# Eight-batch two-layer kernel: the first (gelu) experts run dense for batch 0 only, and by dispatched tiles of 256 token rows for batches 1 to 7

## The chip, the core and the metric

The kernel runs on one NeuronCore of a Trainium2 chip. The metric is device time in microseconds (us) of one execution, from three runs. The profile is one execution taken by the hardware profiler; its times count from the first instruction. PE is TensorE, PEld its weight loads, DVE is VectorE, ACT ScalarE, POOL GpSimd, and SP (SPq) the queue that issues most DMAs.

## The reference

Input x has 8 batches of 512 tokens of width 256. Two layers follow one another. Each layer normalises x, modulates it by the batch, adds a gated block, normalises and modulates again, and adds a gated mixture of experts:

```
x = x + ga * L0_attn(h)      # a retention (running average of sigmoids) and a 256-1024-256 gelu network
x = x + gb * L0_ffn(h)       # 8 gelu experts, top 2
x = x + ga * L1_attn(h)      # 16-head attention with sigmoid weights
x = x + gb * L1_ffn(h)       # 8 silu experts, top 2, and a shared one
```

The change touches the second line, and what lies on either side of it:

```
gates = jax.nn.softmax(xt @ gate_w, axis=-1)
topk_g, topk_i = jax.lax.top_k(gates, TOP_K)
tok_w = topk_g.sum(axis=-1)
sel = (topk_i[:, :, None] == jnp.arange(NUM_EXPERTS)[None, None, :]).any(axis=1)
h = jax.nn.gelu(jnp.einsum('nd,edh->enh', xt, w1) + b1[:, None, :], approximate=False)
y = jnp.einsum('enh,ehd->end', h, w2) + b2[:, None, :]
out = jnp.einsum('end,ne,n->nd', y, sel.astype(x.dtype), tok_w)
```

Both chosen experts of a token count with the same weight, the sum of its two softmax gates. An expert is 256 by 128 and 128 by 256.

## The kernel before

Four parts run one after the other, with a barrier of all engines between them: retention_part, gelu_experts_part, attention_part, silu_experts_part. x stays on chip (c.x), and so do the features of every batch (c.hT, in the store hT_store). Products are in float32 by three passes over halves: each operand is split into a rounded head and a rest, and `product` issues head by head, head by rest, rest by head. ACT writes a head and DVE subtracts it for the rest.

**Retention part.** One iteration for each batch. PE widens batch b to 1024 features (8 steps), does the retention of batch b+1, and narrows back in four steps (`narrow`). DVE and POOL do the norms around it; POOL's part of a norm is `invert` (two small operations). The routing logits of a batch are made one iteration later. The batches 1 to 6 run in hardware loops.

**Gelu experts part, dense.** Every batch goes through all 8 experts. For expert e, `up` is 6 matmuls of 128x512, ACT applies gelu twice (once to g, once to the head of hidden), DVE makes the rest, `down` is 12 matmuls of 128x256, and DVE adds each of four row tiles to e_acc, weighed by the token's coefficient (zero where the expert isn't chosen). PE does up(e+1) before down(e). In the gaps the batch before is finished: `update_x`, `moments`, `normalise`, eight transposes, `modulate`, and `sum_squares` for the next layer's norm. For the last batch the last steps of this are left to the attention part.

**Attention part.** Before its first iteration comes a run of products, rotations and turnings for batch 0 alone. Each iteration is cut into 16 units; in each, PE makes scores (at_sc_ps), ACT one 128x2048 sigmoid block (at_wide), PE multiplies it by the values (at_o_ps). Between units PE does projections for the next batch and the output of the last one. Engines run in the written order, so a wait holds up all that stands behind it on its engine. POOL scatters rows for the silu experts (`ds.scatter`) and places values.

**Silu experts part.** It is already sparse: rows sorted by expert lie in DRAM (slots_dram), a list of 39 tiles of 256 rows is worked out on DVE, SP reads each tile's place from it (value_load) and loads the rows, and PE turns and multiplies them. The change doesn't touch it; its rows show what some steps of such a scheme cost.

## Time and profile before

| | |
|---|---|
| median of 3 runs | 1575.64 us (1574.94 to 1579.48) |
| the profiled execution's span | 1575.8 us |
| PE busy | 1454.8 us (92%) |
| DVE busy | 1117.6 us (71%) |
| ACT busy | 931.7 us (59%) |
| POOL busy | 368.6 us (23%) |
| mean granted TensorE clock | 0.965 of full |

The profiled execution has no time of its own beside its span. A busy share is a mean over parts with different limits, so the table says only which engine is busiest over all; the stages are read apart. Idle time of an engine counts only where another waits for it.

### The profile page before, as it was taken

To read this page: it belongs to the slowest core of one execution; us is meant where nothing else is said; L and a number is where in the kernel's file an instruction comes from. 1 tells how busy PE (TensorE), PEld (TensorE's weight loads), DVE (VectorE), ACT (ScalarE), POOL (GpSimd) and SP (SyncE) were. 2 spreads that over 40 slices of the span, in tenths; PEclk is the share of its full clock that TensorE was granted. 3 is DMA by queue.
4 is the path that set the end of the run, shared out by engine and by line. 5 is a ranking of instruction groups with operands and counts; after the bars stand their busy time and mean duration, and the time that the engine had idled before them with its cause. 6 is when DMAs were issued, how large, how long until landed. Compare 5 with 4: busy or idle time off the path is not lost. (4 is left out here: it accounts for less than half of the span.)

```text
span 1575.8 us, 29143 instructions
## 1 busy us (share of the span) xinstructions
PE 1454.8 (92%) x10406; PEld 1165.5 (74%) x10406; DVE 1117.6 (71%) x2334; ACT 931.7 (59%) x1174; POOL 368.6 (23%) x382
## 2 busy tenths in 40 slices
PE   6899999878999996899999999969999999999998
PEld 4788888767888884454555545438889999999987
DVE  4667777658887885656775686456568778778768
ACT  2466666524555553767776686754257777777752
POOL 1132222330100110111032233224213333333320
PEclk9899999979999997999999999999999999999999
DMA  8000000210000000220000000101349888888864
GB/s 281 1 1 0 0 0 0 81 42 1 0 0 0 0 0 27 75 90 1 1 26 15 19 30 19 62 32 61 129 133 236 237 228 236 235 230 234 234 155 158
DMA packets 65726, 130.51 MB, mean 83 GB/s; under 512 B 8393, under 2 KB 39026, under 8 KB 65138
## 3 DMA queue, kind: packets, MB, share of 16 engines
q1 hardware_dynamic: 51346, 110.39, 22.5%
q0 software_dynamic: 14304, 19.15, 5.9%
q8 instruction: 44, 0.72, 0.2%
q14 instruction: 32, 0.26, 0.1%
HBM read 97.51 MB, written 32.00 MB: 82 GB/s over the span
## 5 line engine op out<-in xcount | busy, mean ns | idle before, releaser
L1831 ACT ACTIVATE at_wide<-at_sc_ps 128x2048 f32<-128x2048 f32 x128 | 240.6, 1880 | 106.0 <-PE at_sc_ps L1657 104.2
L52 PE MATMUL e_gate_ps<-e_h_parts,e_w 128*128 128x256 f32 (+1 forms) x1128 | 178.5, 306 | 10.0 <-DVE e_w L2549 6.3
L2290 POOL DMA_INDIRECT sums<-e_y,e_row_ids x78 | 121.8, 1562 | 247.6 <-ACT e_y L2495 235.7
L2549 DVE TENSOR_TENSOR e_w<-early,e_w 128x1024 fp32r<-128x1024 f32 x123 | 147.1, 1223 | 43.5 <-ACT e_w L2431 43.5
L52 PE MATMUL e_up_ps<-e_h_parts,e_w 128*128 128x256 f32 (+1 forms) x1128 | 175.4, 303 | 0.0
L52 PEld LDWEIGHTS e_gate_ps<-e_h_parts,e_w 128*128 128x128 f32 x1128 | 156.0, 194 | 18.0 <-DVE e_w L2549 6.5
L52 PEld LDWEIGHTS e_up_ps<-e_h_parts,e_w 128*128 128x128 f32 x1128 | 155.5, 193 | 8.1
L1671 PE MATMUL at_o_ps<-at_wide,at_v_ones 128*32 128x512 f32 x1024 | 140.7, 622 | 0.0
L2386 PE MATMUL e_down_ps<-e_w,e_hidden 128*128 128x256 f32 x936 | 127.9, 286 | 1.1 <-DVE e_hidden L2598 1.1
L2431 ACT ACTIVATE e_w<-early 128x1024 fp32r<-128x1024 f32 x123 | 125.1, 1049 | 2.8 <-DMA early<-in_experts 2.8
L1657 PE MATMUL at_sc_ps<-at_qT,at_kT 32*128 32x512 f32 x1024 | 96.7, 452 | 29.6 <-ACT at_wide L1831 27.7
L2386 PEld LDWEIGHTS e_down_ps<-e_w,e_hidden 128*128 128x128 f32 x936 | 117.3, 191 | 1.3 <-DVE e_hidden L2598 1.3
L52 PE MATMUL e_down_ps<-e_w_down,e_hidden 128*128 128x256 f32 x768 | 105.7, 287 | 8.4 <-DVE e_hidden L1138 8.4
L52 PEld LDWEIGHTS e_down_ps<-e_w_down,e_hidden 128*128 128x128 f32 x768 | 99.3, 192 | 17.8 <-DVE e_hidden L1138 7.9
L1149 DVE SCALAR_TENSOR_TENSOR e_acc<-e_down_ps,coef,e_acc 128x256 f32<-128x256 f32 x256 | 105.8, 475 | 3.2 <-PE e_down_ps L52 2.7
L52 PE MATMUL in_ps<-h_parts,w_in 128*128 128x512 f32 x384 | 101.3, 412 | 7.0 <-ACT hidden L604 4.3
L52 PE MATMUL e_up_ps<-layer_h_parts,e_w_up 128*128 128x512 f32 x384 | 105.2, 410 | 2.0 <-DVE e_w_up L1189 2.0
L515 PE MATMUL out_ps<-w_out,hidden 128*128 128x256 f32 x768 | 99.9, 286 | 0.0
L52 PEld LDWEIGHTS in_ps<-h_parts,w_in 128*128 128x128 f32 x384 | 70.0, 192 | 36.5 <-ACT hidden L604 18.7
L1381 POOL DMA_INDIRECT slots<-shared,ds_slots x64 | 69.9, 1092 | 115.6 <-DVE e_hidden L2580 46.6
L515 PEld LDWEIGHTS out_ps<-w_out,hidden 128*128 128x128 f32 x768 | 96.3, 193 | 0.0
L1657 PEld LDWEIGHTS at_sc_ps<-at_qT,at_kT 32*128 32x128 f32 x1024 | 39.7, 186 | 69.7 <-issue 34.5
(357 smaller groups left out, 2644.2 us busy)
## 6 DMA issues: line engine op xcount, KB each, us to landing
early<-in_experts SPq DMA_DIRECT2D x123, 512.0 KB, 4.6
e_rows_in<-slots SPq DMA_DIRECT2D x39, 272.0 KB, 3.6
sums<-shared SPq DMA_DIRECT2D x17, 256.0 KB, 3.4
x<-in_L_attn_x SPq DMA_DIRECT2D x8, 512.0 KB, 9.7
gate<-gates SPq DMA_DIRECT2D x4, 1024.0 KB, 4.7
slots<-shared SPq DMA_DIRECT2D x15, 272.0 KB, 3.3
out<-x SPq DMA_DIRECT2D x7, 512.0 KB, 3.6
e_sums<-sums SPq DMA_DIRECT2D x4, 512.0 KB, 4.9
```

What stands on the lines that cost most here:

```text
L52: last = pe.matmul(out, left(i), right(j), start=n == 0, stop=n == len(steps) - 1)
L515: last = nc.tensor.matmul(to, hidden[:, i, m, cols], w_out[:, j, m, :], start=False, stop=m == MC - 1 and n == 2)
L1149: last = nc.vector.scalar_tensor_tensor(out=acc[:, t, :], in0=rows_of(down_ps[e % 2], t), scalar=c.coef[:, b, t, e:e + 1], in1=acc[:, t, : ...
L1381: pool.indirect_dma_start(self.c.slots_dram, bass.IndirectOffsetOnAxis(ap=self.slots[:, which, at:at + 1], axis=0), self.rows[:, b % 2, t, ...
L1657: last = nc.tensor.matmul(sc_ps[:, m, :], kT[strip, 2 * pair + quad % 2, k * P:(k + 1) * P], qT[strip, part, 2 * pair + quad % 2, :], star ...
L1671: last = nc.tensor.matmul(o_ps[MW * m:MW * (m + 1), quad % 2, :], v_ones[:, par, k, at:at + MW], wide[:, u % 2, m * S:(m + 1) * S], start= ...
L1831: nc.scalar.activation(wide[:, u % 2, :], sc_ps[:].rearrange("p n s -> p (n s)"), ACT.Sigmoid, scale=float(HD) ** -0.5).then_inc(sig_done, 1)
L2290: pool.indirect_dma_start(c.sums_dram[:, :], bass.IndirectOffsetOnAxis(ap=row_ids[:, j % 2, t:t + 1], axis=0), y[:, j % 2, t, :], None, co ...
L2386: last = nc.tensor.matmul(down_ps[:, buf, t * D:(t + 1) * D], hidden[:, p, i, at:at + P], down_rows(1 - buf, r, i), start=i == 0 and m == ...
L2431: nc.scalar.activation(w[:, buf, HEAD, q], raw[:, q], ACT.Copy).then_inc(w_head_done, 1)
L2549: nc.vector.tensor_tensor(w[:, buf, REST, q], raw[:, q], w[:, buf, HEAD, q].bitcast(F32), ALU.subtract).then_inc(w_split, 1)
```

## The change

Batch 0 goes through the dense scheme as before. For batches 1 to 7:

- In the retention part DVE chooses each batch's two experts a token (`choose`), PE ranks the tokens (`rank`, two matmuls), DVE turns ranks into slots (`place_tokens`), PE turns the features back to rows (`make_rows`, 8 transposes), ACT keeps them (`keep_rows`), and POOL scatters them into rows0_dram, 8 indirect DMAs for each batch. Batches 1 to 5 go there; the scatters of 6 and 7 are in the experts part. Loops are unrolled. `keep_hT` on POOL goes.
- In the experts part DVE lists 35 tiles (`list_tiles`). SP pads the end of each expert's region and loads each tile's rows. For each tile POOL copies that expert's weights (128x1024) and its bias rows (128x256) into one of two buffers, PE turns the rows (4 transposes), widens (6 matmuls of 128x256) and narrows (6 of 128x256), ACT does a copy and two gelus, DVE two rests and the bias (`keep_y`), and SP stores the tile's result in y0_dram. Batch 0's tail is spread over the first 12 tiles.
- In the attention part POOL gathers the two results of every token (`gather`, 8 indirect DMAs for each batch; the second four add to the first), DVE weighs and adds them to x (`combine`), and the norm, the turning, the modulation and the sum of squares that stood in the experts part follow: moments_in, normalise_in, in_by_feature, modulate_in, square, sum_squares, keep_sums. Batch n's is done one iteration before its projections; those of batch 1 and the gathers of batch 2 stand before iteration 0. The gate is loaded batch by batch.

The core of the diff:

```diff
--- before.py
+++ after.py
+SPARSE = B - 1
+TILES0 = (2 * SPARSE * S - E) // TS + E
+REGION0 = SPARSE * S + TS
+UNUSED0 = TILES0 - 2 * SPARSE * S // TS
...
+    def rank(self, pe, b, to):
+        pe.wait_ge(self.chosen, b)
+        nc, i = self.nc, b - 1
+        nc.tensor.matmul(to, self.earlier[:], self.c.coef[:, b].rearrange("p t e -> p (t e)"), start=True, stop=False)
+        nc.tensor.matmul(to, self.every[:], self.pm[:, NT * i:NT * (i + 1)].rearrange("p t e -> p (t e)"),
+                         start=False, stop=True).then_inc(self.ranked, 1)
+
...
+    def scatter(self, pool, b, ns):
+        for n in ns:
+            if n == 0:
+                pool.wait_ge(self.placed, b)
+                pool.wait_ge(self.rows_kept, 2 * b)
+            t, which = n // 2, n % 2
+            at = NT * (b - 1) + t
+            pool.indirect_dma_start(self.c.rows0_dram, bass.IndirectOffsetOnAxis(ap=self.slots[:, which, at:at + 1], axis=0),
+                                    self.rows[:, b % 2, t, :], None).then_inc(self.scattered[b % 2], 16)
+
...
+                def scatter(b, *ns):
+                    if b >= 1:
+                        fd.scatter(pool, b, ns)
+
                 def iteration(b, first=False, x_left=True):
                     if not first:
                         norm_2.invert(pool, b - 1)
                         norm_next.invert(pool, b - 1)
-                        keep_hT(b - 1)
+                    scatter(b - 2, 0, 1, 2, 3)
                     if x_left:
                         norm_x.invert(pool, b + 2)
+                    scatter(b - 2, 4)
                     norm_1.invert(pool, b + 1)
+                    scatter(b - 2, 5, 6, 7)
                     gate_tables(b, b + 2)
 
                 norm_x.invert(pool, 0)
@@ -448,14 +565,15 @@
...
+                def load_rows(j):
+                    if j >= ROW_BUFS:
+                        sp.wait_ge(tile_turned, j - ROW_BUFS + 1)
+                    at = sp.value_load(tile_base[0:1, j:j + 1], min_val=0, max_val=E * REGION0 + (UNUSED0 - 1) * TS)
+                    sp.dma_start(rows_in[:, j % ROW_BUFS], c.rows0_dram[bass.ds(at, TS)].rearrange("(p t) r -> p t r", p=P)
+                                 ).then_inc(rows_loaded[j % ROW_BUFS], 16)
+
+                def store_y(j):
+                    sp.wait_ge(tile_kept, j + 1)
+                    sp.dma_start(c.y0_dram[j * TS:(j + 1) * TS].rearrange("(p t) r -> p t r", p=P), y[:, j % Y_BUFS]
+                                 ).then_inc(fd.y_stored[j % Y_BUFS], 16)
+
...
+                sp.wait_ge(listed, 1)
+                for e in range(E):
+                    at = sp.value_load(pads[0:1, e:e + 1], min_val=0, max_val=E * REGION0 - TS)
+                    sp.dma_start(c.rows0_dram[bass.ds(at, TS)].rearrange("(p t) r -> p t r", p=P), empty).then_inc(padded, 16)
+                fd.all_scattered(sp)
+                sp.wait_ge(padded, 16 * (UNUSED0 + E))
+                for j in range(ROW_BUFS):
...
+                fd.scatter(pool, B - 2, range(2 * NT))
...
+                def copy_weights(j):
+                    e = pool.value_load(tile_expert[0:1, j:j + 1], min_val=0, max_val=E - 1)
+                    if j >= 2:
+                        pool.wait_ge(tile_down, j - 1)
+                    nc.gpsimd.tensor_copy(tile_w[:, j % 2:j % 2 + 1].rearrange("p x u i d -> p (x u i d)"),
+                                          w[:, bass.ds(e, 1)].rearrange("p x u i d -> p (x u i d)")).then_inc(tile_w_copied, 1)
+                    if j >= 2:
+                        pool.wait_ge(tile_kept, j - 1)
+                    pool.wait_ge(b_rows_loaded, 16)
+                    nc.gpsimd.tensor_copy(tile_b[:, j % 2:j % 2 + 1].rearrange("p x d -> p (x d)"),
+                                          b_rows[:, bass.ds(e, 1)].rearrange("p x d -> p (x d)")).then_inc(tile_b_copied, 1)
+
+                pool.wait_ge(listed, 1)
+                pool.wait_ge(up_split, len(CHUNKS))
+                pool.wait_ge(down_split, len(CHUNKS))
+                for j in range(TILES0):
+                    copy_weights(j)
...
+                def tile_widen(j):
+                    pe.wait_ge(tile_w_copied, j + 1)
+                    if j < 2:
+                        pe.wait_ge(g_done, E)
+                    else:
+                        pe.wait_ge(tile_gelu, j - 1)
+                    pe.wait_ge(tile_split, j + 1)
+                    product(nc.tensor, up_ps[:, j % 2, 0:TS],
+                            [(lambda i, k=k: tile_w[:, j % 2, 0, i, k * P:(k + 1) * P],
+                              lambda i, k=k: tile_h[:, j % 2, i, k, :]) for k in range(KC)]).then_inc(tile_up, 1)
+
+                def tile_narrow(j):
+                    if j < 2:
+                        pe.wait_ge(acc_done, E)
+                    else:
+                        pe.wait_ge(tile_kept, j - 1)
+                    pe.wait_ge(tile_rest, j + 1)
+                    for t in range(TT):
+                        last = product(nc.tensor, down_ps[j % 2][:, 0, t * D:(t + 1) * D],
+                                       [(lambda i: tile_hidden[:, j % 2, i, t * P:(t + 1) * P],
+                                         lambda i: tile_w[:, j % 2, 1, i, :])])
+                    last.then_inc(tile_down, 1)
 
                 pe.wait_ge(tables_set, 1)
...
+                turn(0)
+                turn(1)
+                tile_widen(0)
+                for j in range(TILES0):
+                    if j + 2 < TILES0:
+                        turn(j + 2)
+                    if j + 1 < TILES0:
+                        tile_widen(j + 1)
+                    tile_narrow(j)
+                    if j == 6:
...
+                def tile_gelus(j):
+                    act.wait_ge(tile_up, j + 1)
+                    if j >= 2:
+                        act.wait_ge(tile_down, j - 1)
+                    nc.scalar.activation(g[:, j % 2, 0:TS], up_ps[:, j % 2, 0:TS], ACT.Gelu, bias=tile_bias[:, j:j + 1])
+                    nc.scalar.activation(tile_hidden[:, j % 2, HEAD], up_ps[:, j % 2, 0:TS], ACT.Gelu,
+                                         bias=tile_bias[:, j:j + 1]).then_inc(tile_gelu, 1)
...
+                def rest_of_rows(j):
+                    dve.wait_ge(tile_head, j + 1)
+                    nc.vector.tensor_tensor(tile_h[:, j % 2, REST], tp_ps[:, j % 2, :].rearrange("p (k s) -> p k s", k=KC),
+                                            tile_h[:, j % 2, HEAD].bitcast(F32), ALU.subtract).then_inc(tile_split, 1)
+
+                def rest_of_tile(j):
+                    dve.wait_ge(tile_gelu, j + 1)
+                    nc.vector.tensor_tensor(tile_hidden[:, j % 2, REST], g[:, j % 2, 0:TS],
+                                            tile_hidden[:, j % 2, HEAD].bitcast(F32), ALU.subtract).then_inc(tile_rest, 1)
+
+                def keep_y(j):
+                    dve.wait_ge(tile_b_copied, j + 1)
+                    if j < Y_BUFS:
+                        dve.wait_ge(next_weights_split, 4)
+                    else:
+                        dve.wait_ge(fd.y_stored[j % Y_BUFS], 16 * (j // Y_BUFS))
+                    dve.wait_ge(tile_down, j + 1)
+                    nc.vector.tensor_tensor(y[:, j % Y_BUFS], down_ps[j % 2][:, 0, :].rearrange("p (t d) -> p t d", t=TT),
+                                            tile_b[:, j % 2].unsqueeze(1).broadcast_to([P, TT, D]), ALU.add).then_inc(tile_kept, 1)
...
+                    elif e == 5:
+                        fd.place_tokens(dve, LAST, rank_ps)
+                        list_tiles()
...
+                def gather(n, which):
+
+                    if n >= B:
+                        return
+                    if which:
+                        pool.wait_ge(got[n % 2], got_by(n) + 16 * NT)
+                    for t in range(NT):
+                        at = NT * (n - 1) + t
+                        pool.indirect_dma_start(rows_by_token(c, n)[:, t, :], None, c.y0_dram,
+                                                bass.IndirectOffsetOnAxis(ap=fd.slots[:, which, at:at + 1], axis=0),
+                                                compute_op=ALU.add if which else ALU.bypass).then_inc(got[n % 2], 16)
+
...
+                gather(1, 1)
+                norm_in.invert(pool, 0)
+                gather(2, 0)
+                gather(2, 1)
...
+                def combine(n):
+
+                    dve.wait_ge(got[n % 2], got_by(n) + 16 * 2 * NT)
+                    for t in range(NT):
+                        at = NT * (n - 1) + t
+                        last = nc.vector.scalar_tensor_tensor(out=rows_by_token(c, n)[:, t, :], in0=rows_by_token(c, n)[:, t, :],
+                                                              scalar=fd.token_weight[:, at:at + 1], in1=c.gate[:, n, :],
+                                                              op0=ALU.mult, op1=ALU.mult)
+                    last.then_inc(weighted, 1)
+                    dve.wait_ge(weighted, n)
+                    nc.vector.tensor_tensor(c.x[:, n], c.x[:, n], rows_by_token(c, n), ALU.add).then_inc(combined, 1)
...
```

The order of instructions on POOL, in the experts part. Before, from the last weights of the attention (w_o) on; e_coef is the copy of a batch's coefficients:

```order
L852 TENSOR_TENSOR w_o<-at_w_raw,w_o 128x512
L924 COPY e_coef<-coef 128x32
L222 TENSOR_TENSOR e_norm_shifted<-e_norm_moments,e_eps 128x4
L225 TENSOR_TENSOR e_norm_inv_std<-e_norm_shifted,neg_half 128x4
L941 UNCONDITIONAL_BRANCH
```

The changed kernel at the same place, with the first of the 35 tiles and the start of the second; rows is rows0_dram, e_tile_w a tile's weights, e_tile_b its bias rows:

```order
L1002 TENSOR_TENSOR w_o<-hT,w_o 128x512
L405 DMA rows<-hT,ds_slots 32512x256 x8
L1152 TENSOR_LOAD shared
L1152 ISA x2
L1155 ISA
L1155 COPY e_tile_w<-e_w 128x1024
L1160 ISA
L1160 COPY e_tile_b<-hT 128x256
L1152 TENSOR_LOAD shared
```

POOL had a few small operations for each batch here; now it has the eight scatters of batch 7 and then, for each tile, a register read and two copies.

PE at the loop over experts. Before:

```order
L52 MATMUL e_down_ps<-e_w_down,e_hidden 128x256 x12
L52 MATMUL e_up_ps<-layer_h_parts,e_w_up 128x512 x6
L52 MATMUL e_down_ps<-e_w_down,e_hidden 128x256 x12
L52 MATMUL e_up_ps<-layer_h_parts,e_w_up 128x512 x6
L52 MATMUL e_down_ps<-e_w_down,e_hidden 128x256 x12
```

Now, from the last dense expert to the first tiles (a round turns tile j+2, widens j+1, narrows j):

```order
L56 MATMUL e_down_ps<-e_w,e_hidden 128x256 x24
L1256 MATMUL e_tp_ps<-ident,hT 128x128 x8
L56 MATMUL e_up_ps<-e_tile_h,e_tile_w 128x256 x6
L1256 MATMUL e_tp_ps<-ident,hT 128x128 x4
L56 MATMUL e_up_ps<-e_tile_h,e_tile_w 128x256 x6
L56 MATMUL e_down_ps<-e_tile_w,e_tile_hidden 128x256 x6
L1256 MATMUL e_tp_ps<-ident,hT 128x128 x4
L56 MATMUL e_up_ps<-e_tile_h,e_tile_w 128x256 x6
```

A tile has 12 products of 128x256 where an expert of a batch had 6 of 128x512 and 12 of 128x256, and one operand of each is now e_tile_w, which POOL writes.

DVE before the attention's first iteration, in the rotation of batch 0. Before:

```order
L1935 TENSOR_TENSOR hT<-early 128x64x8 x2
L1945 SCALAR_TENSOR_TENSOR at_qT<-at_sc_ps,at_sign,at_qT 128x4x128
L1952 SCALAR_TENSOR_TENSOR at_kT<-at_sc_ps,at_odd,at_kT 128x4x128
L1945 SCALAR_TENSOR_TENSOR at_qT<-at_sc_ps,at_sign,at_qT 128x4x128
L1952 SCALAR_TENSOR_TENSOR at_kT<-at_sc_ps,at_odd,at_kT 128x4x128
L1907 TENSOR_TENSOR layer_h_parts<-hT,layer_h_parts 128x1024
```

Now (at L2462 hT is the gathered rows of batch 1, at the second L2462 those of batch 2, at L2477 the normalised rows):

```order
L2462 SCALAR_TENSOR_TENSOR hT<-hT,fd_token_weight,gate 128x256 x4
L2467 TENSOR_TENSOR x<-x,hT 128x1024
L214 BN_STATS at_norm_in_stats<-x 128x6 x4
L222 BN_AGGR at_norm_in_moments<-at_norm_in_stats 128x2 x4
L2375 TENSOR_TENSOR hT<-early 128x64x8 x2
L2385 SCALAR_TENSOR_TENSOR at_qT<-at_sc_ps,at_sign,at_qT 128x4x128
L2392 SCALAR_TENSOR_TENSOR at_kT<-at_sc_ps,at_odd,at_kT 128x4x128
L2477 TENSOR_SCALAR hT<-x,at_norm_in_moments,at_norm_in_inv_std 128x2x128 x4
L2385 SCALAR_TENSOR_TENSOR at_qT<-at_sc_ps,at_sign,at_qT 128x4x128
L2392 SCALAR_TENSOR_TENSOR at_kT<-at_sc_ps,at_odd,at_kT 128x4x128
L2485 TENSOR_SCALAR mean_square<-at_a_ps 128x4
L2345 TENSOR_TENSOR layer_h_parts<-hT,layer_h_parts 128x1024
```

The combining and normalising of batch 1 stand among the last steps of batch 0's queries and keys; the combining of batch 2 follows as the first work of iteration 0.

## Rows read from the trace of the kernel before

**Rows 1.** Windows: us, busy of PE, PEld, DVE, ACT, POOL, clock, DMA, GB/s
```profile
337.50:377.40 39.90, 35.89 (x189) 29.86 (x190) 28.24 (x62) 21.26 (x31) 13.04 (x18) 0.81 0.15 42
377.40:592.80 215.40, 199.12 (x1252) 170.82 (x1250) 177.09 (x418) 115.27 (x168) 19.83 (x27) 0.98 0.00 0
592.80:620.20 27.40, 17.70 (x88) 14.55 (x88) 20.51 (x27) 7.25 (x12) 3.76 (x14) 0.75 0.11 39
620.20:1040.30 420.10, 389.18 (x3164) 200.16 (x3168) 268.18 (x630) 297.87 (x229) 92.77 (x97) 0.98 0.09 33
```

**Rows 2.** Timeline, PE, dense experts: start, us, what
```profile
478.13 1.56 PE L52 MATMUL e_up_ps<-layer_h_parts,e_w_up 128*128 128x512 f32 x6
479.53 1.58 PE L52 MATMUL e_down_ps<-e_w_down,e_hidden 128*128 128x256 f32 x12
```

**Rows 3.** Timeline, PE, tiles of the silu experts
```profile
1172.62 1.60 PE L52 MATMUL e_up_ps<-e_h_parts,e_w 128*128 128x256 f32 x12
1174.06 0.60 PE L2333 MATMUL e_tp_ps<-ident,e_rows_in 128*128 128x128 f32 x4
1174.41 1.68 PE L2386 MATMUL e_down_ps<-e_w,e_hidden 128*128 128x256 f32 x12
```

**Rows 4.** Groups by line: busy us, mean ns, idle before
```profile
L1149 DVE SCALAR_TENSOR_TENSOR e_acc<-e_down_ps,coef,e_acc 128x256 f32<-128x256 f32 x256 | 105.8, 475 | 3.2 <-PE e_down_ps L52 2.7
...
L1543 POOL COPY at_v_ones<-hT 128x1024 f32<-128x1024 f32 x8 | 8.4, 1045 | 177.1 <-DVE hT L1960 177.1
```

**Rows 5.** Timeline, hand-over from POOL and to POOL
```profile
337.67 0.21 POOL L924 COPY e_coef<-coef 128x32 f32<-128x32 f32 x1
338.02 1.01 PE L977 MATMUL e_tp_ps<-ident,e_coef 128*8 128x128 f32 x4 [6.54 <-POOL e_coef L924]
...
598.35 0.69 DVE L1960 TENSOR_TENSOR hT<-at_a_ps,at_v_bias 128x512 f32<-128x512 f32 x1 [1.80 <-PE at_a_ps L52]
599.31 1.05 POOL L1543 COPY at_v_ones<-hT 128x1024 f32<-128x1024 f32 x1 [3.55 <-DVE hT L1960]
```

**Rows 6.** Timeline, scatters, pads and row loads of the silu experts
```profile
1084.54 0.96 POOL L1381 DMA_INDIRECT slots<-shared,ds_slots  x1 [0.30 <-issue]
1085.80 0.96 POOL L1381 DMA_INDIRECT slots<-shared,ds_slots  x1 [0.30 <-issue]
...
1122.36 9.72 SPq L2227 DMA_DIRECT2D slots<-shared  x8
...
1151.94 1.69 POOL L1381 DMA_INDIRECT slots<-shared,ds_slots  x1 [1.03 <-DVE e_hidden L2580]
...
1155.91 1.48 SPq L2207 DMA_DIRECT2D e_rows_in<-slots  x2
...
1158.55 0.61 PE L2333 MATMUL e_tp_ps<-ident,e_rows_in 128*128 128x128 f32 x4
```

**Rows 7.** Timeline, DVE and POOL together, and DVE alone
```profile
740.28 1.47 DVE L1920 TENSOR_TENSOR early<-early,at_cos_sin 128x1024 f32<-128x1024 f32 x1
740.82 3.20 POOL L1534 TENSOR_TENSOR x<-x,at_gate_bias 128x1024 f32<-128x1024 f32 x1
...
764.88 1.23 DVE L1920 TENSOR_TENSOR early<-early,at_cos_sin 128x1024 f32<-128x1024 f32 x1
```

**Rows 8.** Timeline, attention: sigmoid blocks and what PE does between
```profile
731.54 1.88 ACT L1831 ACTIVATE at_wide<-at_sc_ps 128x2048 f32<-128x2048 f32 x1 [1.41 <-PE at_sc_ps L1657]
...
732.85 1.85 PE L1715 MATMUL at_a_ps<-at_router_w,hT 128*128 128x8 f32 x16
...
735.48 1.88 ACT L1831 ACTIVATE at_wide<-at_sc_ps 128x2048 f32<-128x2048 f32 x1 [2.06 <-PE at_sc_ps L1657]
```

**Rows 9.** Windows around PE's pauses before the attention's first iteration
```profile
608.60:612.00 3.40, 1.08 (x8) 0.86 (x8) 3.37 (x6) 0.39 (x1) 0.00 (x0) 1.00 0.01 2
612.00:615.40 3.40, 0.05 (x2) 0.05 (x1) 3.40 (x6) 0.78 (x2) 0.00 (x0) 0.56 0.00 0
```

**Rows 10.** Timeline, DVE, one batch's choosing
```profile
775.06 1.30 DVE L864 TENSOR_TENSOR shared<-ds_probs 128x28 f32<-128x28 f32 x14
```

928 lines of the change are left out of this document (615 added, 313 removed).

## The prediction

> **What bounds the kernel now.** I read the run by its parts, in the order in which they follow, and in each asked which engine has least room. The windows by stage [rows 1] show the dense experts in two stretches: batch 0 (39.9 us, PE 35.9 busy, clock 0.81) and batches 1 to 7 (215.4 us, PE 199.1 busy, clock 0.98). PE is busy 92% of the second, DVE 82%, POOL 9%. So this stage is PE's, and its 255.3 us are what the change attacks. The stretch from the attention's start to its first sigmoid block is 27.4 us with DVE busy 20.5: a chain through DVE. The attention after it (420.1 us) has PE busy 389.2, or 93%, DVE 64%, POOL 22%. PE is the engine with no room there too, so work that goes to it from elsewhere is paid for; DVE and POOL work mostly isn't, unless it stands in the wrong place.
>
> **The work saved.** An expert of a batch costs PE 1.40 us for 6 products of 512 columns [rows 2], and its 12 products of 256 columns as much again: 2.8 us, 56 times for batches 1 to 7. A tile has 12 products of 256 columns, which take 1.44 us in the silu tiles, and 4 transposes, 0.35 us [rows 3]: 1.8 us, 35 times, or 63 us. If PE set the pace of the tiles, 215 us would become 63. I don't think it does.
>
> **The pace of a tile.** The weights are double-buffered, but POOL's copy of tile j+2's weights waits until tile j is narrowed, and PE's next product is the widening of j+2, with only four transposes ahead of it. So the copy lies on the path of every tile. Its length: a POOL copy of 128x1024 takes 1.05 us [rows 4]; from the end of the awaited DVE operation to the start of such a copy it is 599.31 - 599.04 = 0.27 us, and from the end of a POOL copy to the PE instruction that waits for it 338.02 - 337.88 = 0.14 us [rows 5]. That makes 1.46 us, and the transposes (0.35) fit inside it. Then PE widens and narrows, 0.72 us each at the silu tiles' pace [rows 3], plus 0.16 us because the last product must be through (a row of 12 lasts 1.60, its successor starts after 1.44). Period 3.06 us.
>
> To that comes contention. DVE's rest of a tile (two operands in SBUF) starts when the gelus end, about when POOL's next copy starts. A DVE operation of that kind beside a POOL one took 1.47 us and one alone 1.23 [rows 7]: 0.24 us for twice the columns and more. I take 0.15 us, between nothing and 0.24: 3.2 us a tile. The Trainium skill, "SBUF — State Buffer", section "SBUF: two separate sides", says that a two-input DVE operation and a GpSimd operation that reads SBUF hold the shared ports exclusively, so that the second waits for the whole first. By that the term would be the whole rest operation, estimated at 0.4 us, and the sum 9 us higher; the rows show less than a full wait.
>
> POOL's other work for a tile: a bias copy, between nothing and a quarter of 1.05 plus a start, 0.4 us by the 0.21 us of a 32-column copy [rows 5], and a register read. A read, its arithmetic and a DMA issue take SP 9.72/8 = 1.2 us [rows 6], so at most 1.2 for the read. Sum with the copy 2.7 us, just under 3.2. DVE has three operations of 256 to 512 columns, below 1.8 us by 0.475 for 256 [rows 4]; batch 0's tail adds about 12 us of DVE over the first 12 tiles, for which I put 3 us of stalls.
>
> **The hand-over from batch 0 to the tiles.** Today two experts' rounds (5.6 us) follow the sixth accumulation, so it ends about 34.3 us into the part [rows 1, 2]. The new DVE work ahead of it (placing batch 6, choosing batch 7: 15 comparisons, 1.30 us for 14 [rows 10], and some small ones; placing batch 7) is about 6 us; I take 5 as shown: 39.3. Then DVE lists the tiles (estimate 4.3, some 14 short operations of 0.2 to 0.5), SP reads and issues eight pads, 1.0 + 9.7 us [rows 6], which land 2.6 us later, as a row load does (1155.91 to 1158.55). Batch 7's scatters run beside this: 8 at the 1.26 us step of [rows 6], and 2.3 us from the last one's end (1153.63) to the first row load, in all 12.4 against the pads' 17.6, so the pads end last. Then SP reads the first tile's place and loads it, 0.9 + 2.6: PE turns tile 0 at 39.3 + 4.3 + 10.7 + 2.6 + 3.5 = 60.4 us. PE has by then stood still for some 14 us, so the first tile goes at the half clock (0.56 in a window after such a pause [rows 9]): 6.5 us to its end.
>
> Part: 60.4 + 6.5 + 34 x 3.2 + 3 + 0.8 (the last keep_y) = 179.5 us, against 255.3: **-75.8 us**.
>
> **The retention part** gets 48 transposes on PE (six batches), 4.2 us at [rows 3]'s pace, and 5 rankings, between nothing and 0.35 each: **+6 us**. DVE's choosing (3 to 4 us a batch) stands where DVE waits for ACT's scaling, and POOL's scatters (10 us of 37) where POOL waits for moments; both at nothing. If that cover were gone, choosing would cost 4 us for six batches, 24.
>
> **The attention.** Before the first sigmoid block: POOL can gather batch 1 only when the last result is stored, 2.6 us after the barrier; two sets of four at 1.26 us with the memsets between end about 19 us in, and land at 19 + 2.3, near where DVE comes to combine them (18.6 us in, after two of four rotations). On DVE then stand 4 x 0.475 + 1.23 and the moments (1.8), and behind them transposes, two modulations, a square, all ahead of the sigmoid on ACT. I take +7 us, between 5 (DVE's share alone) and 12 (if nothing overlaps). The gathers of batch 2 end some 40 us in and hold DVE at the head of iteration 0: +3. In each later iteration PE gets 16 one-column products for the sum of squares. A block of 16 such small ones is 1.85 us and the unit with it lasts 3.94 us (731.54 to 735.48), with POOL and DVE idle around it [rows 8]; 8 transposes add 0.7, of which half falls into a pause, and a square on ACT adds up to 1.0. That is 3.3 us for each of six; less 2.9 us for the same steps of the last batch that stood there before: +18. Sum **+28 us**. DVE's extra 6.5 us an iteration lie in its 36% idle.
>
> **Sum:** 1575.8 - 75.8 + 6 + 28 = **1534 us**. The profiled span, 1575.8, is within 0.2 us of the median, 1575.64, so nothing is shifted.
>
> **Rivals.**
> - *POOL sets the pace of the tiles.* If the register read takes 2 us on POOL and can't run under a copy, a tile is 2.0 + 1.05 + 0.4 + 0.5 for hand-overs = 3.95 us: +25, 1559 us. For it: the trace has no register read on POOL. Against it: SP's is under 1.2 [rows 6]. Likewise if attention and retention stall twice as much as I say: +34, 1568. Together 0.25.
> - *The additions hide.* If the new PE work falls into PE's 7% pauses and the tiles run at 2.9 us: -10 and -15, about 1508. Chance 0.15. A tile at PE's own 1.8 us is excluded by the wait for the narrowing.
> - *The clock drops: slower.* PE would be busy 1.8 of 3.2 us, 56%, and idle in each tile. At the half clock a tile is 1.46 + 2 x 1.44 + 0.16 + 0.15 = 4.65 us, +49: 1583. It decides from 4.4 us a tile on, where the gain is gone. For it: a window with PE busy 1.08 of 3.40 was followed by one at 0.56 [rows 9]. Against it: that window itself, busy a third, still had clock 1.00. The Trainium skill, "TensorE: Matmul & The Clock Gate", section "The HAM clock gate", has the clock throttled by default and released by activity; by that a half-busy PE is at risk, and the sum is this rival's. Chance 0.10.
> - *No change*, the gain eaten by waits at the two hand-overs: it would take 42 us beyond those counted. Chance 0.05.
> - My forecast, 1515 to 1553: 0.45.
>
> **Numbers.** About 0.3% (5 us) is what a measurement of this kernel can tell from no change. The range reaches to the first two rivals and leaves out the last two: 1500 to 1568. Faster 0.85, same 0.04, slower 0.11.
>
> **What would show it.** Tile steps: starts of the weight copies 3.2 us apart, each behind a narrowing, and PE's idle time ahead of a widening ended by POOL. If a copy follows its register read and not a narrowing, the first rival holds; if the products of 256 columns last twice as long, the clock did. The hand-over: a PE pause of about 14 us ended by the row load, after pads and not after scatters. The attention: first sigmoid block 34 us after the part's start, and 55 to 56 us an iteration for 52.5. The prediction fails if an engine waits in a place I took for covered: DVE's choosing ahead of rest_h1, or POOL's scatters ahead of norm_1.

## The result, and the profile after

The changed kernel takes 1567.93 us (median of 4 runs, 1565.04 to 1574.60) beside 1576.54 us of the kernel before: a ratio of 0.9947, 95% interval 0.9925 to 0.9969. It is faster by 8.6 us or 0.5%; 42 us were forecast. The profiled run is the longest of the four (1574.6 us, span 1572.6). A second profile of the same kernel, taken with the experiments, spans 1566.8 us, near the median, so the sums use the second and the rows here are of the first. Its parts against those of [rows 1]:

| stretch | before | after | forecast | measured |
|---|---|---|---|---|
| to the start of the experts part | 337.5 | 348.3 | +6 | +10.8 |
| experts part | 255.3 | 184.8 | -75.8 | -70.5 |
| attention, to its first sigmoid block | 27.4 | 37.8 | +7 | +10.4 |
| first to last sigmoid block | 420.1 | 457.6 | +21 | +37.5 |
| last sigmoid block to the end | 535.5 | 538.3 | 0 | +2.8 |
| sum | | | -41.8 | -9.0 |

So the saving came about and then went: every term is some us worse, and half of the 33 us missing is in one, the attention's iterations. The windows of the profile after by stage (columns: the stretch in us, its length, busy time of each engine with its instructions, granted clock as a share of 2.4 GHz, DMA share, GB/s) answer to [rows 1]:

```profile
348.20:413.10 64.90, 41.19 (x199) 34.64 (x199) 41.74 (x108) 22.17 (x32) 30.39 (x40) 0.68 0.36 124
413.10:537.60 124.50, 85.38 (x585) 75.75 (x585) 90.67 (x132) 54.95 (x112) 54.19 (x72) 0.91 0.47 155
537.60:574.70 37.10, 20.65 (x100) 16.92 (x100) 25.80 (x43) 9.88 (x14) 22.23 (x30) 0.64 0.22 50
574.70:1034.30 459.60, 421.49 (x3298) 226.96 (x3301) 307.26 (x726) 309.97 (x244) 162.51 (x156) 0.94 0.16 45
```

POOL, busy 9% of the dense experts [rows 1], is busy 44% of the tiles, PE 69%. The attention has 421.5 us of PE work, for 389.2 before: 32 us more, where the products counted in the prediction (1.85 and 0.7 us, six times) make some 15.

The hand-over from batch 0 to the tiles, in the timeline (start, duration, engine, line, operation, output and inputs, in brackets the idle time ahead and what ended it):

```profile
378.91 3.32 DVE L352 TENSOR_TENSOR hT<-logits 128x28 f32<-128x28 f32 x14
...
384.14 3.70 DVE L360 TENSOR_TENSOR hT<-hT,coef 128x8 f32<-128x8 f32 x4
...
388.50 2.93 PE L56 MATMUL e_down_ps<-e_w,e_hidden 128*128 128x256 f32 x12 [7.06 <-DVE e_hidden L1423]
...
394.24 1.07 POOL L405 DMA_INDIRECT rows<-hT,ds_slots  x1 [6.41 <-DVE ds_slots L381]
...
399.00 8.97 SPq L1121 DMA_DIRECT2D rows<-hT  x8
...
410.46 3.69 SPq L1110 DMA_DIRECT2D hT<-rows  x4
...
413.09 1.09 PE L1256 MATMUL e_tp_ps<-ident,hT 128*128 128x128 f32 x4 [10.83 <-DMA hT<-rows]
414.20 0.43 SPq L1126 DMA_DIRECT2D hT<-in_L_ffn_b  x1
...
421.66 0.40 POOL L1160 COPY e_tile_b<-hT 128x256 f32 x1 [15.99 <-DMA hT<-in_L_ffn_b]
...
423.45 0.80 PE L56 MATMUL e_up_ps<-e_tile_h,e_tile_w 128*128 128x256 f32 x2 [5.30 <-POOL e_tile_w L1155]
```

The reader is to see three things. DVE's choice of batch 7 takes 8.9 us and makes PE pause 7.06 us; the 14 comparisons take 3.32 us for 1.30 in [rows 10], since POOL splits the attention's weights beside them (e7_weights_first below). PE turns tile 0 at 413.1, 64.9 us into the part (62.3 in the second profile; forecast 60.4), after a pause ended by the row load, as forecast, though of 10.8 us for some 14. And POOL's bias copy waits 16 us for the load of the bias rows, which SP issued behind four row loads; the second tile's weight copy is queued behind it, and PE's widening waits 5.30 us. That wait I had not seen.

A tile in the steady stretch, on POOL, PE and DVE:

```profile
479.83 1.04 POOL L1155 CAST e_tile_w<-e_w 128x1024 fp32r x1 [0.47 <-PE e_down_ps L56]
...
480.92 0.98 PE L56 MATMUL e_up_ps<-e_tile_h,e_tile_w 128*128 128x256 f32 x6 [0.83 <-POOL e_tile_w L1155]
...
481.74 0.88 PE L56 MATMUL e_down_ps<-e_tile_w,e_tile_hidden 128*128 128x256 f32 x6
...
482.79 1.04 POOL L1155 CAST e_tile_w<-e_w 128x1024 fp32r x1 [0.47 <-PE e_down_ps L56]
482.81 1.30 DVE L1516 TENSOR_TENSOR e_tile_hidden<-e_g,e_tile_hidden 128x256 fp32r<-128x256 f32 x1 [0.47 <-ACT e_tile_hidden L1373]
```

Copies start 2.96 to 2.97 us apart, each 0.47 us of idle behind a narrowing, and PE's 0.83 us of idle ahead of a widening is ended by POOL: the loop narrowing, copy, widening, as forecast. DVE's rest (L1516, two inputs in SBUF) takes 1.30 us beside the copy; the shortest of its 35 took 0.41.

In the attention, PE's units 1 and 2 of the iteration that attends batch 3; they lie in the intervals between the sigmoid blocks of units 2, 3 and 4:

```profile
751.20 1.88 ACT L2261 ACTIVATE at_wide<-at_sc_ps 128x2048 f32<-128x2048 f32 x1
...
752.50 0.31 PE L1700 MATMUL at_a_ps<-coef,shared 128*128 128x32 f32 x2
...
752.64 0.39 PE L1701 MATMUL at_a_ps<-shared 128*128 128x32 f32 x2
...
752.87 1.93 PE L2127 MATMUL at_a_ps<-at_router_w,hT 128*128 128x8 f32 x16
...
754.65 2.40 PE L2145 MATMUL at_a_ps<-at_ones,early 128*128 128x1 f32 x16
...
756.99 1.23 PE L2069 MATMUL at_sc_ps<-at_qT,at_kT 32*128 32x512 f32 x8
...
758.14 1.94 PE L2083 MATMUL at_o_ps<-at_wide,at_v_ones 128*32 128x512 f32 x8
758.32 1.88 ACT L2261 ACTIVATE at_wide<-at_sc_ps 128x2048 f32<-128x2048 f32 x1 [5.25 <-PE at_sc_ps L2069]
...
760.01 2.90 PE L56 MATMUL at_a_ps<-w_v,layer_h_parts 128*128 128x256 f32 x12
...
765.08 1.88 ACT L2261 ACTIVATE at_wide<-at_sc_ps 128x2048 f32<-128x2048 f32 x1 [4.76 <-PE at_sc_ps L2069]
```

Ranking, routing and the new sum of squares (L2145) stand in a row, 4.5 us of narrow products with no idle time between them. What follows takes more: scores 1.23 us for 0.74, attention products 1.94 for 1.06, values' products 2.90 for 1.69 (L56 of another iteration). Between the sigmoid blocks lie 7.12 and 6.76 us, where before they were 4.38 and 4.97 in this iteration, and 3.94 with the routing alone [rows 8]. The sums themselves are slow here too. Their 16 records take 1.84 us where they stand alone, in the iteration of batch 1, and up to 3.04 us in that of batch 5 (second profile):

```profile
632.77 1.84 PE L2145 MATMUL at_a_ps<-at_ones,early 128*128 128x1 f32 x16
...
872.46 3.04 PE L2145 MATMUL at_a_ps<-at_ones,early 128*128 128x1 f32 x16
```

### The profile page after: what moved, and what is told of

The parts are those of the page before. It is cut to its first block and busy times, and to the rows that moved or that the text cites. A ratio compares the mean times of both kernels' runs of the same rounds, so it can differ in the third digit from the quotient of the medians.

```text
span 1572.6 us, 28181 instructions
## 1 busy us (share of the span) xinstructions
PE 1390.5 (88%) x9960; PEld 1114.6 (71%) x9960; DVE 1117.0 (71%) x2352; ACT 893.5 (57%) x1148; POOL 547.1 (35%) x561
## 5 line engine op out<-in xcount | busy, mean ns | idle before, releaser
L56 PE MATMUL e_gate_ps<-e_h_parts,e_w 128*128 128x256 f32 (+1 forms) x1128 | 178.5, 306 | 9.4 <-DVE e_w L3022 5.9
L56 PE MATMUL e_up_ps<-e_h_parts,e_w 128*128 128x256 f32 (+1 forms) x1128 | 175.9, 303 | 0.0
L56 PEld LDWEIGHTS e_gate_ps<-e_h_parts,e_w 128*128 128x128 f32 x1128 | 156.0, 194 | 17.5 <-DVE e_w L3022 6.1
L56 PEld LDWEIGHTS e_up_ps<-e_h_parts,e_w 128*128 128x128 f32 x1128 | 155.8, 193 | 8.2
L2083 PE MATMUL at_o_ps<-at_wide,at_v_ones 128*32 128x512 f32 x1024 | 145.7, 643 | 0.0
L56 PE MATMUL in_ps<-h_parts,w_in 128*128 128x512 f32 x384 | 103.4, 417 | 9.0 <-DVE h_parts L842 6.5
L56 PEld LDWEIGHTS in_ps<-h_parts,w_in 128*128 128x128 f32 x384 | 71.4, 195 | 37.2 <-ACT hidden L741 14.7
L1948 POOL DMA_INDIRECT hT<-y,ds_slots x56 | 76.2, 1360 | 25.2 <-issue 15.3
L2957 ACT ACTIVATE e_hidden<-e_gu_silu 128x512 fp32r<-128x512 f32 x78 | 49.3, 632 | 58.7 <-DVE e_gu_silu L3066 57.1
L405 POOL DMA_INDIRECT rows<-hT,ds_slots x56 | 60.7, 1084 | 52.9 <-DVE ds_slots L381 38.7
L3071 DVE TENSOR_TENSOR e_hidden<-e_gu_silu,e_hidden 128x512 fp32r<-128x512 f32 x78 | 54.0, 693 | 28.2 <-ACT e_hidden L2957 27.9
```

Of the source, the lines that this page charges most:

```text
L56: last = pe.matmul(out, left(i), right(j), start=n == 0, stop=n == len(steps) - 1)
L405: pool.indirect_dma_start(self.c.rows0_dram, bass.IndirectOffsetOnAxis(ap=self.slots[:, which, at:at + 1], axis=0), self.rows[:, b % 2, t, ...
L1948: pool.indirect_dma_start(rows_by_token(c, n)[:, t, :], None, c.y0_dram, bass.IndirectOffsetOnAxis(ap=fd.slots[:, which, at:at + 1], axis= ...
L2083: last = nc.tensor.matmul(o_ps[MW * m:MW * (m + 1), quad % 2, :], v_ones[:, par, k, at:at + MW], wide[:, u % 2, m * S:(m + 1) * S], start= ...
```

## Experiments

All ratios are against the kernel before on the same chip. The changed kernel itself, run again beside the last group but one, gave 1569.3 us, ratio 0.9958 (0.9943 to 0.9972). "Interval k" is the time from the sigmoid block of unit k to the next, and iteration n attends batch n. Over the eight iterations, against before, interval 2 grew by 14.7 us, interval 7 by 10.1, 15 by 3.7, 3 by 2.8, 11 by 2.3, and the rest by 3.9.

> The changed kernel itself, beside the kernel before on this chip, so that the differences of the other kernels can be read against it: 1566 to 1572 us.

### The sums in the attention

```diff
+ if n >= 2:
+     nc.tensor.matmul(a_ps[:, 1, 96:100], squares[:, 0, 0:P], c.ident[:, 0:NT], start=True, stop=True)
+     return
```

> Leaves out 7 of the 8 one-column products (on the trace 14 of 16 records) with which the attention sums the squares of batches 2 to 7; their sums are then not the reference's. Theory A (clock): these products cost 2.4 to 2.8 us themselves, and in the iterations of batches 3 to 6, where they stand behind the routing and ranking products, they also make a stretch of some 5 us of small products after which the scores take 1.23 us for 0.74, the attention products 1.94 for 1.06 and the values' products 2.5 to 2.9 for 1.69. Then the interval between the sigmoid blocks of units 2 and 3 falls from 7.1-7.8 to about 4.9 us, the next one from 6.1-6.8 to about 5, and the time by some 22 us (4 iterations by 4.2, 2 by 2.5) against the changed kernel. Rival B (queues): the iteration is held by the chain keep sums, inverse root on POOL, placing of values, rotation; the products go, the chain stays, and the time falls by the products alone, 12 us, or by less.

Measured 1549.35 us, ratio 0.9820 (0.9794 to 0.9846): 20 to 22 us less than the changed kernel. First to last sigmoid block took 439.8 us for 457.6; interval 2 is 4.2 to 5.0 us in iterations 2 to 6 (before: 3.9 to 4.6). At the full clock the sums take 1.84 to 1.95 us, so the products left out are worth 7/8 of that, six times: some 10 us, or less, since in iteration 1 PE has a pause there and interval 2 fell by 1.06 us only. The other 8 us or so of the 17.9 are the clock's, on the sums themselves (2.3 to 3.0 us in iterations 3 to 6) and on what follows them. Windows of intervals 2 and 3 while batch 4 is attended, of the changed kernel (second profile), then of this one:

```profile
807.27:814.77 7.50, 7.50 (x60) 6.02 (x56) 2.20 (x12) 1.88 (x2) 0.98 (x1) 0.79 0.04 10
814.77:821.18 6.41, 6.41 (x38) 3.82 (x37) 2.87 (x10) 1.99 (x2) 2.51 (x6) 0.72 0.01 3
```

```profile
801.41:806.01 4.60, 4.60 (x46) 3.38 (x42) 1.50 (x8) 1.88 (x1) 0.49 (x1) 1.00 0.00 0
806.01:812.23 6.22, 6.22 (x38) 3.90 (x34) 3.31 (x12) 1.99 (x2) 3.00 (x6) 0.73 0.00 0
```

PE counts as busy for all of both. The granted clock of the first is 0.79 (part of it at the lower of its two levels), and 1.00 without the sums. Theory A holds for the sums; the second interval was at 0.73 all the same, so the sums are not what brings that one alone: the kernel before, with ranking and routing alone, has 0.92 and 0.78 in these two intervals.

```diff
  # unit 1, behind route(b - 2, 1)
- sum_squares(b + 1)
  # unit 2, ahead of the values' second half
+ pe.wait_ge(logits_kept, b - 1); pe.wait_ge(ds.placed, b - 2)
+ sum_squares(b + 1)
  # DVE: keep_sums(n) goes behind ds.place_tokens
```

> The same 8 sum products of each batch stand one unit later, behind the scores and the attention products of unit 2, so that no stretch has all the small products together; nothing is left out. Theory A (clock): the stretch of small products falls from about 5 us to 2.5 twice, the scores, attention and values' products go back to 0.74, 1.06 and 1.7 us, and the two intervals that now take 13.3 to 13.9 us take about 12: the time falls by about 8 us against the changed kernel. Rival B (queues): inverse roots come 2 us later on POOL, the rotations wait for them, and the time is the same or up to 6 us longer. A third way: the clock falls in any case, since the two intervals together have as few wide products as before; then the time is the same.

Measured 1576.54 us, ratio 0.9995 (0.9981 to 1.0008): 6 to 8 us more than the changed kernel. Interval 2 is 4.38 us in iterations 3 to 6, but interval 3 is 8.4 or 11.4 (6.9 in iteration 2). In the iteration of batch 5, where it is 11.4:

```profile
877.18 3.57 PE L2145 MATMUL at_a_ps<-at_ones,early 128*128 128x1 f32 x16
...
881.01 2.93 PE L56 MATMUL at_a_ps<-w_v,layer_h_parts 128*128 128x256 f32 x12 [0.25 <-DVE mean_square L2489]
...
883.74 2.70 PE L56 MATMUL at_a_ps<-w_qk,layer_h_parts 128*128 128x512 f32 x6
```

The clock falls anyway, and now under the sums (3.57 us for 1.95 in iteration 2, where the granted clock of the interval is 1.00; here it is 0.55), the values' products (2.93) and the first query products (2.70 for 1.56): the third way, and worse than it. DVE waits for PE there, and PE has 0.25 us of idle time, behind the kept sums, in 11.4 us, so rival B is out. Spreading the narrow products did not help here; what did was to have less of them.

```diff
- 8 products: out 128x1 <- squares[128x128], ones
+ for k in range(KC):
+     nc.tensor.matmul(a_ps[:, 0, :], ones_r[:].broadcast_to([P, P]), o_parts[:, REST, k], ...)
+ # ACT: the squares go to o_parts' rest, once that is free; PE waits for the sums ahead of the queries
+ # DVE: times the identity, reduce, then as before, and all of it behind ds.place_tokens
```

> The sum of squares of batches 2 to 7 is made by 2 products of 512 columns of a column of ones (broadcast) with the squares, which give each sum on all partitions, in place of 8 products of one column; DVE takes each partition's own sum with the identity (two more operations, some 1.4 us); nothing is left out. Theory (clock, and small products): PE spends about 0.6 us in the place of 2.4 to 3.6, the interval behind unit 2 goes to 4.7-5.3 us (from 7.1-7.8) in the iterations of batches 3 to 6, and the time falls by 13 to 20 us against the changed kernel, most of what leaving out the sums gave. Rival: DVE's 1.4 us more ahead of the rotations become the wait of the query and key products, and the gain is under 8 us.

Measured 1558.88 us, ratio 0.9884 (0.9867 to 0.9900): 10 to 12 us less than the changed kernel. First to last block took 443.3 us, 14.3 less; interval 2 is 4.5 to 5.4 us in iterations 2 to 6. On PE the sum is now one row:

```profile
806.74 0.71 PE L2150 MATMUL at_a_ps<-at_o_parts,at_ones_r 128*128 128x512 f32 x2
...
807.86 0.68 DVE L2500 TENSOR_TENSOR early<-at_a_ps,ident 128x512 f32<-128x512 f32 x1
```

The rival is out: the gain is above its 8 us, so DVE's two operations (0.68 and 0.69 us) mostly fall into its waits. The ratio fell a little less than expected; interval 1 came out at 5.3 us in iterations 4 and 6 for 3.7, at a granted clock of 0.68.

### The order on DVE and ACT in the attention

Interval 7 of iteration 4 in the changed kernel (second profile). The four normalising operations stand ahead of the output's rest, and PE waits for that rest:

```profile
828.36 3.56 DVE L2477 TENSOR_SCALAR hT<-x,at_norm_in_moments,at_norm_in_inv_std 128x256 f32<-128x256 f32 x4
831.84 1.21 DVE L2425 TENSOR_TENSOR at_o_parts<-at_a_ps,at_o_parts 128x1024 fp32r<-128x1024 f32 x1
...
833.10 1.68 PE L56 MATMUL at_a_ps<-w_o,at_o_parts 128*128 128x256 f32 x12 [1.70 <-DVE at_o_parts L2425]
```

```diff
  # DVE
+ moments_in(m)       # ahead of the kept sums
  keep_logits(b - 2, 1); ds.place_tokens(...)
- moments_in(m)
+ normalise_in(m)     # ahead of keep_values(n, 1)
...
- normalise_in(m)     # ahead of output_rest(p)
  # POOL: the root of the norm goes ahead of that of the sums
```

> DVE takes the moments of the coming batch ahead of the sums and normalises it before it keeps the second half of the values, where it now waits for PE, and POOL inverts in that order; nothing is left out. Theory: in the iterations of batches 3, 4 and 5 the four normalising operations (3.1 to 3.6 us beside POOL's addition of the bias) stand ahead of the output's rest and hold PE's projection: interval 7 takes 5.5 us for 3.3. It goes back to 3.3 to 3.7: minus 6 us against the changed kernel. Rival: the normalising then delays the values and the rotations, which end the wait of PE one or two units later: no change or up to 6 us longer.

Measured 1567.94 us, ratio 0.9936 (0.9916 to 0.9957), no difference from the changed kernel that counts. The mechanism is shown: interval 7 fell from 5.48 to 3.69-3.73 us in iterations 3 to 5, and the sum over interval 7 by 4.3 us (iteration 0 took 1 us more). But interval 1, 3.73 us in iterations 4 to 6, became 5.1 to 5.3, and its sum grew by 4.2, at granted clocks of 0.69 to 0.73 for 1.00. That the one follows from the other is not shown. e5_halves and e6_bias_first, whose edits lie outside the attention, have 5.24 us in one and in two of these three intervals, and c1_best, which has the early normalising too, keeps both: 3.7 us in interval 7 and 3.73 in interval 1.

```diff
- square(b + 2)                       # ACT, unit 15
+ pool: c.hT[:, :, b + 2] * c.hT[:, :, b + 2] -> squares   # near unit 11
+ dve: wait_ge(squares_made, b), ahead of keep_values(b, 0)
```

> In the attention POOL squares the coming batch (one multiplication of 128x1024, near unit 11) and not ACT at unit 15; nothing is left out. Theory: ACT's square (1.04 us) stands ahead of the sigmoid block of the next iteration and makes the interval behind unit 15 3.84 us for 2.9 in five iterations; it goes back to 2.9: 4 to 5 us less. Rival: POOL's multiplication beside DVE's operations slows DVE by what it takes, or holds POOL's scatters and the values' placing: no change or up to 5 us more.

Measured 1567.03 us, ratio 0.9927 (0.9902 to 0.9952): no more than 5 us less, which the two 95% intervals don't tell from nothing, and first to last block no shorter (458.2 us). Interval 15 is 3.0 us in iterations 1, 2 and 5, as the theory says, but 14 is 3.7 to 4.5 there, and 15 is 7.0 and 6.2 in iterations 3 and 4, where PE waited 2.9 and 2.5 us for DVE, whose four normalising operations took 3.7 and 3.8 us beside POOL. The rival holds.

### The tiles and the hand-over

```diff
- pool.wait_ge(tile_down, j - 1); copy of w[:, e] to tile_w[:, j % 2]
+ for u, read in enumerate((tile_up, tile_down)):
+     pool.wait_ge(read, j - 1)
+     copy of w[:, e, u] to tile_w[:, j % 2, u]
```

> POOL copies a tile's up weights as soon as the widening two tiles earlier is through, and its down weights once that tile's narrowing is; nothing is left out. Theory: the pace of 2.97 us a tile is the loop narrowing, copy of 128x1024 (1.04 us), widening, with two hand-overs; with the up weights copied a product earlier only half a copy could lie on the path, and that one has a widening as cover. Then PE (1.8 us) or DVE (three operations, 1.75 us) sets the pace, 2.0 to 2.4 us with hand-overs, and the tiles take 33 x 0.6 to 0.9 = 20 to 30 us less. Rival: POOL itself is near its end (two copies of 0.5, the bias copy 0.4, a register read that no row shows and waits of 0.2 each make 2.6 to 3 us), and the pace stays at 2.7 us or more: less than 10 us.

Measured 1549.24 us, ratio 0.9828 (0.9809 to 0.9848): 20 us less. From tile 0 to the attention 102.6 us for 122.5; a tile takes 2.36 us:

```profile
480.23 0.40 POOL L1161 COPY e_tile_b<-hT 128x256 f32 x1 [0.31 <-DVE hT L1528]
...
480.92 1.36 POOL L1156 CAST e_tile_w<-e_w 128x512 fp32r x2 [0.29 <-issue]
...
481.58 0.98 PE L56 MATMUL e_up_ps<-e_tile_h,e_tile_w 128*128 128x256 f32 x6 [0.22 <-POOL e_tile_w L1156]
...
483.94 0.98 PE L56 MATMUL e_up_ps<-e_tile_h,e_tile_w 128*128 128x256 f32 x6 [0.22 <-POOL e_tile_w L1156]
```

The theory holds, and at 2.36 us the rival's limit is reached: POOL has 0.40 and 1.36 us of copies and two gaps of 0.3, and idles no more than that. The first of the gaps ends with DVE's `keep_y`, so whether POOL alone or the round through `keep_y` and the bias copy now sets the pace is not told apart. The first rival of the prediction (POOL's register read sets the pace) is out: a read costs at most the 0.29 us gap ahead of a copy.

```diff
+ next_weights(pool)
  fd.scatter(pool, B - 2, range(2 * NT))
  ... iotas and their copies
- next_weights(pool)
  fd.scatter(pool, LAST, range(2 * NT))
```

> POOL splits the attention's weights before it scatters the rows of batch 6, as the kernel before had it at that place, and not behind; nothing is left out. Theory: the choosing of batch 7 on DVE then runs beside scatters and not beside POOL's split: the 14 comparisons go from 3.32 us to 1.3-1.5, the four additions from 3.70 to 0.9, and PE's pause of 7.1 us ahead of the narrowing at 388.5 us goes to under 2; the first tile is turned 4 to 5 us earlier, at 60 us from the start of the part for 64.9. Rival: it is the scatters and loads behind it that end last (batch 7's scatters begin only when batch 6's are through), and the first tile is turned at the same time within 1 us.

Measured 1563.34 us, ratio 0.9905 (0.9889 to 0.9922): 8 us less by the ratios, 4 by the two profiles' experts parts (180.5 us for 184.8). The 14 comparisons take 1.33 us, the additions 0.89, PE's pause is 1.17, and tile 0 is turned 58.3 us into the part for 62.3:

```profile
379.31 1.33 DVE L352 TENSOR_TENSOR hT<-logits 128x28 f32<-128x28 f32 x14
...
383.01 1.68 PE L56 MATMUL e_down_ps<-e_w,e_hidden 128*128 128x256 f32 x12 [1.17 <-DVE e_hidden L1423]
```

```diff
+ sp.dma_start(b_rows, ...)      # ahead of load_rows(0)
  for j in range(ROW_BUFS): load_rows(j)
- sp.dma_start(b_rows, ...)
```

> The load of the down biases' rows (which every tile's bias copy on POOL waits for) is issued ahead of the first four loads of tile rows and not behind them; nothing is left out. Theory: POOL's first bias copy waits 16 us for that load (from 405.7 to 421.7 us), and the second tile's weight copy stands behind it in POOL's queue, so PE's widening of the second tile waits 5.3 us; the load comes about 4 us earlier, PE's wait goes, the first row load comes 1.2 us later: minus 3 to 5 us. Rival: another wait of the first tiles (rows, half clock) takes its place: within 1.5 us of no change.

Measured 1568.12 us, ratio 0.9940 (0.9919 to 0.9960): the rival. PE's wait of 5 to 6 us is gone, but the first rows landed 5 us later (tile 0 at 415.65 for 410.60). On SP's queue what was issued first landed first: the bias copy starts at 414.41 us, ahead of tile 0, and in the changed kernel some 9 us behind it.

### The retention part

The changed kernel in the iteration from 249.9 to 287.5 us (second profile). The 14 comparisons run beside POOL's work on gate and bias:

```profile
259.11 5.37 DVE L352 TENSOR_TENSOR hT<-logits 128x28 f32<-128x28 f32 x14
...
261.95 2.44 POOL L544 TENSOR_TENSOR x<-x,shared 128x1024 f32<-128x1024 f32 x1
...
266.12 1.22 DVE L842 TENSOR_TENSOR h_parts<-h,h_parts 128x1024 fp32r<-128x1024 f32 x1
...
267.39 4.69 PE L56 MATMUL in_ps<-h_parts,w_in 128*128 128x512 f32 x18 [1.37 <-DVE h_parts L842]
```

```diff
- fd.choose(dve, b - 1)
  rest_h1(b + 1)
+ fd.choose(dve, b - 1)
```

> In the retention part DVE chooses the experts of a batch behind the rest of h1 and not ahead of it; nothing is left out. Theory: the choosing (7 us beside POOL's bias work, its 14 comparisons 5.4 us where they take 1.3 elsewhere) ends 1.1 us too late for the rest of h1 in each of five iterations, and PE's wait ahead of the widening falls from 1.4-2.4 to 0.2-1.3 us: the part ends 5 to 6 us earlier. Rival: the 2 us more of an iteration are PE's own new products (8 transposes and a ranking), and the choosing only moves the wait to the update of x: no change within 2 us.

Measured 1576.56 us, ratio 0.9994 (0.9979 to 1.0009): 6 to 7 us more. The iterations take 38.2 to 38.6 us for 36.4 and 37.6, and the part ends 6 us later. The theory's mechanism is there and its remedy fails. Beside no POOL work the comparisons take 1.31 us and the rest of h1 1.23, and PE's wait ahead of the widening is gone in four of five iterations; but behind them the update of x and the placing come later, and PE now waits 1.4 to 1.7 us an iteration for the placing of a batch (ds_slots), and 6.4 us for 3.0 in the last.

```diff
  scatter(b - 2, 5, 6, 7)
+ pool.wait_ge(fd.chosen, b - 1)
  gate_tables(b, b + 2)
```

> In the retention part POOL begins its work on gate and bias (0.8, 0.7 and 2.4 us) only when DVE has chosen the experts of the batch; nothing is left out. Theory (DVE and POOL slow each other): the 14 comparisons go from 5.37 us to 1.3-1.5, the choosing from 7 us to 3, the rest of h1 begins as soon as ACT has scaled, PE's wait ahead of the widening goes from 1.4-2.4 to 0.2-1.3 us, and an iteration takes 36.5 us for 37.6: 5 us less in all. Rival (arithmetic of DVE): comparisons are slow for another reason, for instance the drains or the rows they read; they stay at 5.4 us, the bias comes later, and an iteration takes 1 to 2 us more.

Measured 1571.55 us, ratio 0.9960 (0.9948 to 0.9973): no change, and iterations of 37.6 us as ever. DVE's rows:

```profile
298.60 1.36 DVE L352 TENSOR_TENSOR hT<-logits 128x28 f32<-128x28 f32 x14
...
300.79 0.89 DVE L360 TENSOR_TENSOR hT<-hT,coef 128x8 f32<-128x8 f32 x4
304.45 2.34 DVE L844 TENSOR_TENSOR h_parts<-h,h_parts 128x1024 fp32r<-128x1024 f32 x1 [2.77 <-ACT h_parts L732]
```

The comparisons do go from 5.37 to 1.36 us, so POOL's work beside them was what slowed them. But POOL's work now lies beside the rest of h1, which takes 2.34 us for 1.22, and PE waits 1.34 us as before (1.37; 2.38 for 2.39 in the iteration of these rows). One of the two operations on the path pays for POOL in either order.

```diff
- for t in (2 * half, 2 * half + 1): for k in range(KC): pe.transpose(...)
+ for t in (2 * half + 1,): for k in (KC - 1,): pe.transpose(...)
```

> Leaves out 6 of the 8 turns per batch by which the retention part makes token rows of batches 1 to 6 (one turn of 128x128 is left in each half, so the rows that are scattered are not the reference's); all waits stay. Theory: an iteration of the retention takes 37.6 us for 35.57 because of PE's own new products on its path: the two blocks of 4 turns 0.35 to 0.47 us each and the ranking's 4 products 0.36. With 3 of 4 turns gone from each block an iteration falls by 0.5 to 0.7 us, to about 37.0, and the part by 3 to 4 us. Rival: the excess is in waits (for the rest of h1, slowed by POOL, and for ACT, which keeps the rows in two operations of 0.6 us), and an iteration stays at 37.6.

Measured 1568.62 us, ratio 0.9945 (0.9930 to 0.9960). An iteration takes 37.24 us for 37.62: 0.38 less, for 0.66 of turns left out (0.47 to 0.14 and 0.36 to 0.03), since the wait for the rest of h1 grew from 1.37 to 1.66 us. So leaving out four fifths of the turns gave back only 0.38 of the 2.05 us by which an iteration grew; the wait takes the rest up.

### Together

The diffs of e5_halves, e7_weights_first, e6_bias_first, e9_wide_sums and e3_norm_early in one kernel:

> Five of the edits together (weights copied in halves, attention weights split ahead of the scatters, bias rows loaded first, sums by two wide products, batch normalised early); nothing is left out. If they add up: tiles 24 us less, first tile turned 6 us earlier, second tile's wait 3 to 5 us less, sums 10 to 16 us less, normalising 3 to 5 us less, in all 46 to 56 us: 1512 to 1522 us, near what was forecast for the change itself. If the clock takes part of it back (a PE that waits less in one unit falls to half in the next, as the early normalising showed), 1525 us or more.

Measured 1521.37 us, ratio 0.9649 (0.9629 to 0.9669): 48 us less than the changed kernel, about what the five gave one by one (47 us by the ratios). By the profiles the experts part takes 24.6 us less and first to last block 25.0 us less, where the sums and the early normalising alone had given 14.3 and 0.6. Intervals 2 and 3 while batch 4 is attended are at the full clock, 4.94 and 4.69 us; in iterations 3 and 5 interval 3 is still 6.1 and 5.8 us:

```profile
773.34:778.28 4.94, 4.94 (x46) 3.38 (x42) 3.40 (x18) 1.88 (x1) 0.56 (x2) 1.00 0.07 24
778.28:782.97 4.69, 4.69 (x38) 2.95 (x34) 4.14 (x11) 2.00 (x2) 2.82 (x3) 1.00 0.00 0
```

```diff
  # SP: clearings of experts 0 to 3 only
+ # ACT's queue: experts 4 to 7
+ at = act.value_load(pads[0:1, e:e + 1], ...)
+ act.dma_start(rows0[at], empty).then_inc(padded, 16)
```

> The five edits together, and the eight clearings of rows behind the experts' lists shared between the queues of SP and ACT, four each; nothing is left out. Theory: with batch 7's scatters now 6 us earlier, the clearings (9 us on SP's queue, then 2.6 us to land) end last before the first row load; with half of them on another queue the first tile is turned 3 to 4 us earlier, at 57 us from the part's start, for about 60.5: 1517 to 1519 us. Rival: the scatters end last, and the first tile is turned at the same time, 1520 to 1522 us.

Measured 1517.47 us, ratio 0.9629 (0.9613 to 0.9645), beside 0.9649 without it: not told apart. Tile 0 is turned 59.3 us into the part for 60.7. SP's clearings take 5.0 us for 9.0 and are issued by 397.7 us, but the last scatter ends at 398.35 and SP goes on at 402.0 (402.8 without the sharing). The time lies where the theory had it, but tile 0 comes 1.4 us earlier and not 3 to 4: by the rows the rival holds, and the scatters end last.

## Why the prediction was wrong

The bound and the saving were right: PE bounds the dense stage, and the part fell by 70.5 us for 75.8, in part by luck, as told below. What failed are the additions: +6 and +28 forecast, +10.8 and +47.9 measured.

One of the rivals had this: "Likewise if attention and retention stall twice as much as I say: +34, 1568". The median is 1567.93. The size of that agreement is luck: attention and retention took 24.7 us more than forecast and not 34, and the rest came from the experts part (5.3) and the last stretch (2.8). The direction and the place are this rival's.

**The attention, the step "That is 3.3 us for each of six", sum +28; measured +47.9.** The trace supports the piece that the price rests on: 16 narrow products last 1.9 us, and so do the sums at the full clock. The error was to price them by a unit in which such a block stood alone. They were put behind ranking and routing, and the clock fell: 17.9 us for the six (e1_one_sum), of which some 8 are clock, for some 12 in my 3.3s. The Trainium skill, "TensorE: Matmul & The Clock Gate", section "The HAM clock gate", says that the clock is throttled by default and that activity releases it. In the tiles, where I used that rule, PE is busy 69% and the clock held for the most part: 1.00 from 466 to 537 us, though 0.66 to 0.83 up to 452 us and 0.72 from 460 to 466, and in the second profile 0.99 to 1.00 from 433 us on. In the attention the rule as it is worded gives no warning: PE counts as busy for all of intervals 2 and 3, and the granted clock was 0.79 and 0.72, for 1.00 and 0.73 without the sums.

Second, the step "DVE's extra 6.5 us an iteration lie in its 36% idle" is wrong in three of the iterations: the normalising stands ahead of the output's rest, and interval 7 takes 5.48 us for 3.27, of which e3_norm_early took 1.8 away (5.3 us in all, and c1_best kept them). A share of idle time says nothing about a queue's order.

Turns and square came near their price: intervals 11 and 15 grew by 0.4 and 0.94 us in iterations 1 to 5, and the turn in interval 7 by 0.4, some 9 us for 8 (0.35 and 1.0, six times). The sum has a slip as well: six times 3.3 less 2.9 is 16.9, not 18. Interval 1 of iterations 2 and 3, 1.5 us longer each, at granted clocks of 0.65 and 0.69, is in none of these terms, and no run tried it.

**Before the first block: +10.4 for +7**, inside its 5 to 12. The gathers end about where DVE comes to them, as forecast, and PE's pause of 7.55 us is ended by DVE's rotation behind the combining. No run tried this stretch by itself.

**The retention: +10.8 for +6.** The step "both at nothing" failed at the place the prediction named as its risk, the choosing ahead of the rest of h1, though not at its price of 24. PE's new products are there (0.83 us of turns, 0.36 of ranking); the rest of the 2.05 us by which three of the iterations grew is the wait for the rest of h1, lengthened by POOL's bias work in whichever order (e10_bias_waits). In the last iteration, which grew by 2.4 us, PE waits 3.18 us for the placing of a batch (2.98 in the second profile); no run took that wait away, and e4_choose_late lengthened it. Another 2.1 us came behind the last routing, and no run tried them. POOL's scatters ahead of norm_1 cost nothing that a run showed.

**The tiles: 122.5 us for 119.1 from tile 0 on.** The pace came out shorter, 2.97 for 3.2: hand-overs of 0.17 and 0.06 us for 0.27 and 0.14, and no contention on the path. The 8 us so won were lost at the start: the bias rows (5 to 6 us) and the lower clock in the first tiles (0.72 from 413 to 430 us in the second profile). That the part's sum came so near is the luck of two errors of one size. The weighing of a rule against [rows 7] went wrong in an instructive way. The Trainium skill, "SBUF — State Buffer", section "SBUF: two separate sides", says that of such a DVE operation and a GpSimd operation the one that starts first holds the shared ports for all of its length, and the other waits. The trace is near that rule: 1.30 us for 0.41 beside a copy of 1.04 that started 0.02 us ahead, 2.34 for 1.22 beside the bias work. I had taken 0.15 us from rows that showed 0.24, and had read them from one side only. In [rows 7] DVE's operation starts 0.54 us ahead of POOL's, and it is POOL's that is long: 3.20 us, where the like one beside no DVE operation took 2.39 in the kernel before. DVE's long operation cost nothing in the tiles, because the narrowing it feeds comes only behind the next widening, and much in the retention, where I had not applied it.

**The hand-over: tile 0 at 62.3 to 64.9 us for 60.4.** The term for DVE's choice (5 us as shown) was short by 4, for POOL beside it (e7_weights_first: 58.3 without), and the others were some 2 too long. That the clearings end last was right in the changed kernel (issued until 408.0 us, scatters until 404.6).

The last stretch's +2.8 us is not explained; the same stretch took 535.5 to 538.8 us in the profiles of the other kernels, so it may be none of the change's.

What stays open is when exactly the clock falls: interval 1 of iterations 5 and 6 took 3.73 or 5.24 us in runs of kernels that do not differ in the attention (the changed kernel, e5_halves, e6_bias_first).

## What to carry to other kernels

Price a block of narrow products together with what already stands around it: here the sums cost some 10 us by themselves and 8 more through the clock, and two products of 512 columns did their work in 0.71 us for 1.84 to 3.04. Where work moves to DVE and POOL, look for pairs with two SBUF inputs beside each other on the path; idle shares hide them. And a loop through a copy can be shortened by splitting the copy by its readers: 0.6 us a tile here, 20 us in all, more than the change as a whole had gained.

## What the runs showed of the hardware

- Products of one column in fp32, 128x128 stationary: 16 records in 1.84 to 1.95 us at the full clock (granted 0.99 to 1.00, iterations 1 and 2), 3.57 in an interval granted 0.55 (e2_sums_later), with PE counted busy nearly throughout. Behind 2.1 us of other narrow products the granted clock was 0.79 over the 7.50 us that hold them, and 1.00 without them (e1_one_sum).
- A DVE operation with two SBUF inputs beside a POOL copy took 1.30 us for 0.41; 14 small comparisons beside POOL's bias work 5.37 for 1.36 (e10_bias_waits).
- The same stretch of PE work can come at either clock: interval 1 of iteration 5 took 3.73 us at 1.00 in the changed kernel and 5.24 at 0.67 in e5_halves, whose edit lies elsewhere.
- A POOL copy whose source is picked by a register starts 0.29 us behind the operation ahead of it (e5_halves).
